# A graph block on one core: layer norm of x ahead of the edges, first projection by chunks of columns

## What is computed

```python
xn = _layernorm(x, axis=-1)
x = x + gnn(xn, edges, ...) + mix(xn[None], ...)[0]
x = x + ffn(_layernorm(x, axis=-1)[None], ...)[0]

def mix(x, Wq, bq, Wk, bk, Wv, bv, Wo, bo):
    q, k, v = x @ Wq.T + bq, x @ Wk.T + bk, x @ Wv.T + bv
    q, k = elu(q) + 1, elu(k) + 1
    kv, z = sum_n(k v), q . sum_n(k) + EPS
    return (q kv / z) @ Wo.T + bo

def gnn(x, edge_index, ...):
    ...
    att = exp(Q[receivers] . K[senders] / sqrt(DK))
    att = att / segment_sum(att, receivers)[receivers]
    agg = scatter_add(att * V[senders], receivers)
    ...
    return x + out
```

## Time and profile before

| what | us |
|---|---|
| median of three runs | 999.07 |
| the profiled execution's own time | 997.54 |
| its span, first to last instruction | 995.8 |
| PE busy (91% of the span) | 911.1 |
| DVE busy (53%) | 525.3 |
| ACT busy (28%) | 275.3 |
| POOL busy (17%) | 166.3 |

### The profile page before, as it was taken

One profiled execution on the slowest core, in us unless ns is written; L12 is line 12 of the kernel. 1 busy time (PEld: TensorE's weight loads), 2 busy tenths in 40 slices (PEclk: granted clock), 3 DMA queues, 4 the chain that ended last, 5 costly groups with the idle time before them and its releaser, 6 DMA issues.

```text
span 995.8 us, 12311 instructions
## 1 busy us (share of the span) xinstructions
PE 911.1 (91%) x4086; PEld 496.4 (50%) x4086; DVE 525.3 (53%) x1366; ACT 275.3 (28%) x471; POOL 166.3 (17%) x199
## 2 busy tenths in 40 slices
PE   2898998899998999999997999999999999979678
PEld 1564444645684333333455776545644555434455
DVE  7785556666665999999666440322222222221731
ACT  2631010201114655656335320011111111111341
POOL 3000000400100000000011526222222222232410
PEclk9999999999998999999998999899999999989789
DMA  9201000001238042210016114388888888884612
GB/s 302 90 3 40 1 1 1 1 0 49 107 107 173 1 104 48 55 43 1 1 52 222 43 46 127 117 310 321 310 292 314 295 314 310 306 305 149 153 42 63
DMA packets 42109, 129.91 MB, mean 130 GB/s; under 512 B 9121, under 2 KB 9603, under 8 KB 41407
## 3 DMA queue, kind: packets, MB, share of 16 engines
q1 hardware_dynamic: 33019, 110.77, 34.4%
q0 software_dynamic: 8576, 18.03, 5.1%
q10 hardware_dynamic: 452, 0.34, 0.1%
HBM read 118.52 MB, written 19.71 MB: 139 GB/s over the span
## 4 chain that ended last, share of the span: by engine, by line
PE 69%; DMA 7%; DVE 6%; issue 6%; POOL 4%; ACT 3%; DVEq 2%; SPq 1%; ACTq 0%; POOLq 0%
PE ps L1468 10%; PE ps L1385 7%; PE ps L1457 7%; PE ps L1610 5%; PE ps L1628 4%; PE ps L1524 4%; PE ps L1412 3%; PE ps L1421 3%; DMA Zg<-z_d,gat 3%; PE ps L1367 3%; PE ps L1536 3%; PE ps L1678 3%; PE ps L1353 2%; POOL list_d L575 2%; PE ps L1493 2%
## 5 line engine op out<-in xcount | busy, mean ns | idle before, releaser
L897 DVE TENSOR_TENSOR att<-ps,C 125x832 f32<-125x832 f32 (+1 forms) x120 | 121.9, 1017 | 16.0 <-ACT ps L1182 12.6
L1182 ACT ACTIVATE ps<-ps 125x832 f32<-125x832 f32 (+1 forms) x120 | 101.7, 849 | 73.7 <-PE ps L1457 73.7
L1468 PE MATMUL ps<-att,V 125*64 125x416 f32 (+1 forms) x480 | 111.7, 544 | 1.7 <-DVE att L897 1.3
L1030 DVE TENSOR_SCALAR hgT<-ps,cols 128x128 f32<-128x128 f32 x148 | 50.5, 404 | 76.2 <-PE ps L1597 67.1
L1457 PE MATMUL ps<-Qst,Kst 128*125 128x416 f32 (+1 forms) x240 | 77.9, 407 | 2.8 <-DMA Qst<-qk_d 2.1
L1036 DVE COPY ehT<-ps 128x256 f32<-128x256 f32 x36 | 15.3, 424 | 122.6 <-PE ps L1618 122.6
L1610 PE MATMUL ps<-W,hgT 128*64 128x256 f32 x576 | 76.7, 412 | 0.0
L1457 PEld LDWEIGHTS ps<-Qst,Kst 128*125 128x125 f32 x240 | 35.8, 188 | 80.9 <-DVE att L897 71.8
L1524 PE MATMUL ps<-hT,Ws_s 128*128 128x250 f32 x320 | 72.4, 381 | 1.0 <-ACT combT L1241 1.0
L1536 PE MATMUL ps<-Ws_s,hsT 128*125 128x512 f32 x160 | 73.3, 598 | 0.0
L1385 PE MATMUL ps<-mW,xnT 128*125 128x512 f32 x160 | 72.2, 594 | 0.0
(11 more groups left out here) (239 smaller groups left out, 1264.2 us busy)
## 6 DMA issues: line engine op xcount, KB each, us to landing
W<-in_W SPq DMA_DIRECT2D x144, 512.0 KB
Kst<-qk_d SPq DMA_DIRECT2D x32, 156.2 KB, 5.6
Qst<-qk_d SPq DMA_DIRECT2D x32, 156.2 KB, 5.9
Yt<-y_d SPq DMA_DIRECT2D x10, 448.0 KB
Ws_s<-in_Ws SPq DMA_DIRECT2D x2, 2048.0 KB, 14.1
qk_d<-qk_hi POOLq DMA_DIRECT2D x4, 625.0 KB, 3.6
qk_d<-qk_lo POOLq DMA_DIRECT2D x4, 625.0 KB, 4.6
z_d<-yz POOLq DMA_DIRECT2D x10, 250.0 KB, 2.7
```

The costliest lines, as they stand in the source:

```text
L897: V_.tensor_tensor(att[:, n % 3, :, 0:w], scores_of(n, w), C[:, s, o:o + w].unsqueeze(1).to_broadcast([P, 2, w]), ALU.mult).then_inc(att_m ...
L1030: i = V_.tensor_scalar(hgT[:, u, k, :], bank(u, 128, 128, k * 128), col("g1", k), col("b1ln", k), ALU.mult, ALU.add)
L1182: S_.activation(b, b, ACT.Exp, scale=float(DK) ** -0.5).then_inc(s_exp, 1)
L1468: k = MM(sums_of(i, 64 * j, 64, w), V[:, s, pair, j:j + 2, :], att[:, n % 3, j, 0:w], start=s == 0, stop=s == T - 1, skip_group_check=True)
```

## The change

- **The head's order.** DVE takes the statistics of the first three pairs of tiles and copies tiles 1 and 3 before it turns to the edges; the last two pairs follow behind them. DVE zeroes three tenths of Cx and POOL seven.
- **Who norms.** ACT normalises all ten tiles. Of XR, POOL makes tiles 0 to 5 (`x_kept`, two scalars per partition, from xs), four ahead of its reduction over the partitions and two behind it; ACT makes tiles 6 to 9.
- **First projection by chunks.** The loop runs over chunks first and feature blocks second. PE transposes tiles 0 to 3, which are what the first chunk of 500 nodes needs, makes two units, and then transposes two more tiles after each of units 1, 2 and 3. `TURNS` is put in that order. ACT's features are moved into a function and start behind the last XR, with the copies of tiles 4, 6 and 8 between them; DVE copies 5 and 7 behind the first one-hots and tile 9 behind the first qT.
- **Counts.** The 12 units have 15 steps instead of 20, the 20 units of the second projection 30 instead of 28, mix_wo 15 instead of 14, gnn_qk 12 as before, gnn_v 8 instead of 6.

The order of PE in the first projection, before: L1367 is a unit, L1353 a count (x8 is two of them), with the ten transposed tiles all ahead of it.

The diff, cut to its core:

```diff
...
 NB = 10
+CX_DVE = 3
+XR_POOL = 6
 WN = W * NB
...
 TURNS = Turns((4, 0, [
-    ("xnT", ["act", "dve"] * 5),
-    ("mix_q", ["act"] * 12),
+    ("xnT", ["act", "dve"] * 2), ("mix_q", ["act"] * 2), ("xnT", ["act", "dve"]), ("mix_q", ["act"]),
+    ("xnT", ["act", "dve"]), ("mix_q", ["act"]), ("xnT", ["act", "dve"]), ("mix_q", ["act"] * 8),
     ("mix_kv", ["dve"] * 20),
...
 def steps_before():
-    after = {"mix_q": [2, 2, 1] * 4, "mix_kv": [1, 2, 1, 1, 2, 1, 2, 1, 1, 2] * 2,
-             "mix_wo": [2, 1, 1, 2, 1, 1, 2, 1, 1, 2], "gnn_qk": [1] * 12, "gnn_v": [1, 0, 1, 0, 1, 0, 1, 0, 1, 1]}
+    after = {"mix_q": [0, 0, 1, 1] + [2, 2, 1, 2] + [1, 2, 1, 2], "mix_kv": [1, 2, 1, 2, 1, 2, 1, 2, 1, 2] * 2,
+             "mix_wo": [2, 1, 2, 1, 2, 1, 2, 1, 2, 1], "gnn_qk": [1] * 12, "gnn_v": [1, 1, 1, 0, 1, 1, 1, 0, 1, 1]}
     table, n = {}, 0
...
         xy_kept = sem("xy_kept")
-        xn_made, xr_set, xr_made = [sem("xn_made0"), sem("xn_made1")], sem("xr_set"), sem("xr_made")
+        xn_made, xr_set, xr_made = sem("xn_made"), sem("xr_set"), sem("xr_made")
         rs_made = sem("rs_made")
...
                            allow_small_or_imprecise_dtypes=True)
-            nc.gpsimd.memset(Cx[:, NB // 2:, :], 0.0)
+            nc.gpsimd.memset(Cx[:, CX_DVE:, :], 0.0)
             gp.drain().then_inc(cx_zero, 1)
+            def x_kept(t):
+                gp.wait_ge(rs_made, t // 2 + 1)
+                nc.gpsimd.tensor_scalar(XR[:, t, :], xs[:, t, :], r1[:, t:t + 1], nb[:, t:t + 1], ALU.mult, ALU.add).then_inc(xr_set, 1)
+            for t in range(4):
+                x_kept(t)
             gp.wait_ge(ends_local, 1)
...
             gp.drain().then_inc(ends_made, 1)
+            for t in range(4, XR_POOL):
+                x_kept(t)
             gp.wait_ge(act_read, TURNS.group_read("xnT", 8)[1])
...
                 return V_.tensor_scalar(dst, src, mvt[:, t, 0:1], rs[:, t:t + 1], ALU.subtract, ALU.mult)
-            V_.memset(Cx[:, 0:NB // 2, :], 0.0)
-            v.wait_ge(edges_in, 16 * 2 * len(PARTS))
-            V_.tensor_single_scalar(e_h[:, 0, :], e_i[:, 0, :], 7, ALU.logical_shift_right)
...
-            v.drain().then_inc(ends_local, 1)
-            v.wait_ge(consts, 1)
+            V_.memset(Cx[:, 0:CX_DVE, :], 0.0)
             def x_stats(i):
...
                 stats(xs, mv, (2 * i, 2 * i + 1), ln_var)
-            def x_norm(i):
+            def x_scales(i):
                 v.wait_ge(ln_std, i + 1)
...
                 v.drain().then_inc(rs_made, 1)
-                t = 2 * i + 1
-                normalise(xn[:, t, :], xs[:, t, :], mv, t).then_inc(xn_made[1], 1)
             def xnT_read(t):
...
             x_stats(0)
-            for i in range(1, 5):
-                x_stats(i)
-                x_norm(i - 1)
-                if i >= 2:
-                    xnT_read(2 * i - 3)
-            x_norm(4)
-            xnT_read(7)
-            xnT_read(9)
+            x_stats(1)
+            x_scales(0)
+            x_scales(1)
+            x_stats(2)
+            xnT_read(1)
+            xnT_read(3)
+            v.wait_ge(edges_in, 16 * 2 * len(PARTS))
+            V_.tensor_single_scalar(e_h[:, 0, :], e_i[:, 0, :], 7, ALU.logical_shift_right)
...
+            v.drain().then_inc(ends_local, 1)
+            x_scales(2)
+            x_stats(3)
+            x_stats(4)
+            x_scales(3)
+            x_scales(4)
             v.wait_ge(ends_made, 1)
...
             one_hots(1, EG)
+            xnT_read(5)
+            xnT_read(7)
             v.wait_ge(cx_zero, 1)
             v.wait_ge(xr_set, T)
-            for m in range(KD):
-                for c, (o, n) in enumerate(CHUNKS):
-                    i = 3 * m + c
+            for c, (o, n) in enumerate(CHUNKS):
+                for m in range(KD):
+                    i = KD * c + m
                     counted_before("mix_q", i)
...
                                             ALU.min, ALU.add).then_inc(qT_made, 1)
+                    if i == 0:
+                        xnT_read(9)
             v.wait_ge(rows_in, 16 * len(ROWS))
...
                 a.wait_ge(rs_made, i + 1)
-                t = 2 * i
-                S_.activation(xn[:, t, :], xs[:, t, :], ACT.Identity, bias=nb[:, t:t + 1], scale=rs[:, t:t + 1]).then_inc(xn_made[0], 1)
+                for t in (2 * i, 2 * i + 1):
+                    S_.activation(xn[:, t, :], xs[:, t, :], ACT.Identity, bias=nb[:, t:t + 1], scale=rs[:, t:t + 1]).then_inc(xn_made, 1)
+            def features(i):
+                c, m = divmod(i, KD)
+                n = CHUNKS[c][1]
+                reads("mix_q", i)
+                if i >= 2:
+                    a.wait_ge(qT_made, i - 1)
+                b = bank(TURNS.bank("mix_q", i), n)
+                S_.activation(eq[:, i % 2, 0:n], b, ACT.Exp, bias=col("mbq", m))
+                S_.activation(rq[:, i % 2, 0:n], b, ACT.Relu, bias=col("mbq", m)).then_inc(act_read, 1)
+                a.drain().then_inc(feat_q, 1)
             a.wait_ge(consts, 1)
...
             x_std(0)
-            for i in range(1, 5):
-                x_std(i)
-                x_norm(i - 1)
-                if i >= 2:
-                    xnT_read(2 * i - 4)
+            x_norm(0)
+            x_std(1)
+            x_norm(1)
+            xnT_read(0)
+            x_std(2)
+            xnT_read(2)
+            x_norm(2)
+            x_std(3)
+            x_std(4)
+            x_norm(3)
             x_norm(4)
+            for t in range(XR_POOL, T):
+                S_.activation(XR[:, t, :], xs[:, t, :], ACT.Identity, bias=nb[:, t:t + 1], scale=r1[:, t:t + 1]).then_inc(xr_set, 1)
+            a.wait_ge(cols_in, 16)
+            a.wait_ge(ends_local, 1)
+            features(0)
+            features(1)
+            xnT_read(4)
+            features(2)
             xnT_read(6)
             xnT_read(8)
-            for t in range(T):
-                S_.activation(XR[:, t, :], xs[:, t, :], ACT.Identity, bias=nb[:, t:t + 1], scale=r1[:, t:t + 1]).then_inc(xr_set, 1)
-            a.wait_ge(cols_in, 16)
-            for m in range(KD):
-                for c, (o, n) in enumerate(CHUNKS):
-                    i = 3 * m + c
-                    reads("mix_q", i)
-                    if i >= 2:
-                        a.wait_ge(qT_made, i - 1)
-                    b = bank(TURNS.bank("mix_q", i), n)
-                    S_.activation(eq[:, i % 2, 0:n], b, ACT.Exp, bias=col("mbq", m))
-                    S_.activation(rq[:, i % 2, 0:n], b, ACT.Relu, bias=col("mbq", m)).then_inc(act_read, 1)
-                    a.drain().then_inc(feat_q, 1)
+            for i in range(3, 12):
+                features(i)
             a.wait_ge(qT_made, 12)
...
                 pe.wait_ge(act_read if who == "act" else dve_read, count)
+            def x_transposed(tiles):
+                for t in tiles:
+                    pe.wait_ge(xn_made, t + 1)
+                    b = turn("xnT", t)
+                    for k in range(KD):
+                        i = nc.tensor.transpose(bank(b, P, 128, k * P), xn[:, t, k:D:KD], ident[0:P, 0:P])
+                    i.then_inc(filled, 1)
             pe.wait_ge(consts, 1)
-            for t in range(T):
-                pe.wait_ge(xn_made[t % 2], t // 2 + 1)
-                b = turn("xnT", t)
-                for k in range(KD):
-                    i = nc.tensor.transpose(bank(b, P, 128, k * P), xn[:, t, k:D:KD], ident[0:P, 0:P])
-                i.then_inc(filled, 1)
-            read_by_now("xnT", 8)
-            read_by_now("xnT", 9)
+            x_transposed(range(4))
+            read_by_now("xnT", 2)
+            read_by_now("xnT", 3)
             pe.wait_ge(mwq_in, 16)
...
                     counts(g % SLOTS, 4 + g % 2)
-            for m in range(KD):
-                for c, (o, n) in enumerate(CHUNKS):
-                    b = turn("mix_q", 3 * m + c)
+            for c, (o, n) in enumerate(CHUNKS):
+                if c:
+                    read_by_now("xnT", (0, 6, 8)[c])
+                    read_by_now("xnT", (0, 7, 9)[c])
+                for m in range(KD):
+                    b = turn("mix_q", KD * c + m)
                     for k in range(KD):
...
                     i.then_inc(filled, 1)
-                    count_after("mix_q", 3 * m + c)
+                    count_after("mix_q", KD * c + m)
+                    if c == 0 and m:
+                        x_transposed((2 * m + 2, 2 * m + 3))
             pe.wait_ge(mwkv_in, 32)
```

More of the change, by code:

```diff
@@ L651, in normalise, with x_stats, xnT_read @@
                 return V_.tensor_scalar(dst, src, mvt[:, t, 0:1], rs[:, t:t + 1], ALU.subtract, ALU.mult)
-            V_.memset(Cx[:, 0:NB // 2, :], 0.0)
+            V_.memset(Cx[:, 0:CX_DVE, :], 0.0)
+            def x_stats(i):
+                v.wait_ge(x_in[i], 16 * len(PARTS))
+                stats(xs, mv, (2 * i, 2 * i + 1), ln_var)
+            def x_scales(i):
+                v.wait_ge(ln_std, i + 1)
+                p = slice(2 * i, 2 * i + 2)
```

(29 more changed lines are left out.)

## The result

The changed kernel takes 1001.47 us in the median of 20 runs (993.93 to 1097.66, a single run at the upper end, the next at 1008.07), the kernel before 995.91 (990.41 to 1001.12, 20 runs). The ratio is 1.0052, with a 95% interval of 1.0029 to 1.0075: slower by 5 us, which is within 1% but clear of noise. The forecast was 1002.0, and +4.3 us against the profiled execution.

The account below looks back on a forecast made before the run. PE was taken to bound the edge stage from 41 us to DVE's last Cx addition. First part -4.1, second projection +6.0, mix_wo +0.35 and gnn_v +2.0 gave +4.3 us, hence 1002.0 us, range 993 to 1009.

Parts of the forecast that it names:

- Start of the projection: First projection: PE's first unit starts at 17.0 us, when the weights land, where before it began after 30 us.
- Where PE stops: First projection, third unit: PE idles 3 to 6 us for ACT's first feature, behind norms and XR, restarting at 31.3.
- Clock: Third unit of the first projection: the idle gap drops PE to half clock, costing 2.2 us.
- The -4.1 us of the first part: Head and first projection: the second projection starts at 69.5 instead of 73.56 us, a gain of 4.1 us.
- Counts in the second projection: Ten second counts behind odd units wait 1.45 us each, 14.5 in all; +6.0 us with two more counts and refill.
- Rival A: Counts of the edge stage: moving them costs nothing, as PE's work is equal; 996.6 us, chance 0.18.
- mix_wo, gnn_v: Later counts: one more in mix_wo costs +0.35 us; two more in gnn_v, with a new wait, cost +2.0 us.
- POOL: Six XR tiles at 1.264 us each by the nearest row, plus more memset: cost nothing, hidden by DVE's stand.
- Rival B: DVE's wait for all XR before the first qT: POOL becomes the bound, from 2.4 us a tile; 1013 us, chance 0.05.
- The sum: Whole kernel: the forecast terms add to +4.3 us, predicting 1002.0 us.
- Rival C: Start: x lands up to 6.4 us late and the clock stays low longer; 1008 us, chance 0.11.
- Rival D: First projection: first feature made at 21, PE runs from 17.0 through, second stage at about 58; 991 us, chance 0.04.

## Why the prediction was right, and where a term was off

**Start of the projection.** 17.0 was forecast, 17.30 came.

**Where PE stops.** The place, the waiting engine and what it waits for are as forecast, 33.2 against 31.3. The term that was mis-sized is the landing of x: "pair 0 at 5 us and one more each 2 us", where the rows show 5.8 and 8.5. DVE's second statistics began at 8.52 where the forecast's own steps give 7.1, 1.4 us later for it, and ACT's last norms at 24.86 instead of 22.9. Two smaller terms, which the prediction put at nothing, are in this: the 0.3 us for which POOL's memset held DVE's scales, and 0.53 us in which DVE stood ahead of the scales of the fourth pair (24.32).

**Clock.** I took 2.2 us; the unit lost 2.4, and the run that kept PE busy shows that the idle time was the cause. The transposes of tiles 6 and 7, behind full units, took 1.0 us where I had 1.0. The Trainium skill, "TensorE: Matmul & The Clock Gate", section "HAM oscillation", says that a wait between bursts of matmuls can send PE back to half clock, so that the next burst starts cold. The traces agree: the third unit was slow in each run with a gap ahead of it (4.50, 6.14, 6.19 and 7.97 us) and at full rate in the two without one and in the one with 0.62 us.

**The -4.1 us of the first part** became -1.5: 1.9 us by the later feature, 0.2 by the clock, the rest in pieces too small to name. More than the size, its owner was wrong. I set the five counts fewer to no one's account and compared the whole with 73.56; the run with the counts alone shows that with the old head those counts give 2.8 us (73.4 to 70.6), 1.7 by their own work and most of the rest by the wait of 1.43 us at 40.41, and that the new head takes up to 1.3 back.

**Counts in the second projection.** Forecast 14.5 us in ten waits, measured 14.7; forecast +6.0 for the stage, measured +6.4 (from the first unit to the end of the last sum). The split by sides, 1.45 and 0.87 us, was checked by moving them: 1.47 and 0.83. Rival A is out, though the run with DVE's steps ahead shows that its hope was sound: an order exists in which the waits vanish.

**mix_wo, gnn_v.** +0.35 forecast and measured; +2.0 forecast, +1.8 measured, with one new wait of 0.9 us.

**Not in the sum:** 0.6 us in the mixer's output between them (176.85 to 198.07 against 171.96 to 192.54). Of it I can say only that DVE stood 0.40 us for PE at 184.50, which has no counterpart before; a stand of 0.43 us at 189.09, with nothing that the profile names, has one (0.42 at 178.30).

**POOL.** Its XR cost nothing, at 0.76 us a tile against my nearest row of 1.264. The Trainium skill, "GPSIMD Engine Reference", section "Engine selection", has one-input work about as fast as on VectorE; DVE's norm of a tile, with one input and two scalars too, took 0.55 us (L651, before), so that is nearer than the row but not met. Rival B is out even with all ten tiles on POOL, though POOL's stands on both sides of the reduction were 6.80 and 8.50 us where it had 5.9 each. What did cost is the longer memset: of the edges' work and the statistics, which the prediction named as what would stretch if the two engines hindered each other, neither did (2.9 us from 16.85, and 1.29 for two), but one instruction of the first scales was held for 0.3 us.

**The sum.** 7.7 us at the end of the edge stage against 4.3, and 5.2 us (2.9 to 7.5) in the timed runs, in which 4.3 lies. That the time came within 1 us of the forecast is partly luck: where the change works, the sum was 3.4 us too low, and of the 7.7 us only 1.5 are left at the end of this profiled pair. Why the timed runs show 5.2 and not 7.7 stays open. Of the signs that the prediction named, the restart (33.2, within 29 to 35) and the waits (14.7 us, above 11) came as forecast; the second projection's first matmul (72.0 against 69 to 70) and the last addition to Cx (297.9 against 294 to 295) did not. Rival C was right in kind and not in size: the feature came 1.9 us late, not 6.4. Rival D was excluded for the reason given.

## What to carry to other kernels

In a queue that runs strictly in order, put work that another engine needs ahead of the wait for something that comes later: the same instructions on DVE cost PE 14.7 us of waiting behind its waits for a unit and 1.6 ahead of them. When a ring of buffers joins two engines, look who empties the oldest buffer and what stands ahead of that in its queue; an early start is worth only what lies before that point. And give each part of a change its own run before crediting it: here the part that looked like the gain was none, and the table beside it made most of the loss.

## What the runs showed of the hardware

- The granted clock reads 1.00 from the start of the profile, but durations say otherwise until PE has worked: two units at 17.30 took 8.83 us, in other runs 6.95 to 9.00, and the first transposes 415 ns instead of 283. At the start of this profile the level has to be read from durations.
- Matmuls whose results nobody reads, put into a gap of 6 us, made the program's second stage start 2.2 us earlier.
- A small scaling of 125x2 elements on DVE took 0.50 us instead of 0.16, because it was held until POOL's memset was over; in five runs it ended at 11.07 or 11.08, with the memset's end at 11.05.
- POOL's form with two scalars per partition took 0.76 us for 512 float32 elements per partition, its two-input addition 1.264 us.
